# Two-layer cross-attention on one core: a logarithm in the softmax shift, and layer 0 features that arrive transposed

## Chip, cores and metric

The kernel runs on one core of a Trainium2 chip. The metric is the device time of one execution in microseconds (us), the median of several runs. All data are fp32. Products that must keep fp32 accuracy are made from a high part (rounded to the fp32r format) and a low part (the rest), in three matmul passes: high x low, low x high, high x high.

## What is computed

Sixteen batches of 256 tokens with 512 features and 16 heads of 32 features. Layer 0 attends from `x` to the 512 rows of the context and `x` together, then runs an MLP over the result. Layer 1 attends from the output of layer 0 to the normalised context. The two attentions are, cut to what matters:

```python
h = jnp.concatenate([x, latents], axis=1)            # layer 0: 512 keys
q = (latents @ q_w + q_b); kv = (h @ kv_w + kv_b)
attn = jnp.where(full_mask, einsum('bkhd,bnhd->bhkn', q, k) / DH, -inf)
attn_out = softmax(attn) @ v;  attn_out = attn_out @ out_w + out_b + residual
out = rmsnorm(attn_out, postnorm_w)                   # then the MLP and the residual
...
a = _layer_norm(audio_kv, ln_gamma, ln_beta)          # layer 1: 256 keys
out = softmax(Q @ K^T * scale) @ V @ Wo.T;  return hidden + tanh(gate) * out
```

## The kernel before

Three blocks follow one another: layer 0's attention, the MLP over 8 chunks of 512 tokens, layer 1's attention. Both attentions are the one function `attention_layer`. Each engine runs its own program in its written order, and semaphores tie them together. One round of the loop works on two batches at once: the first half of attention of batch `a` and the projections of the next batch `p = a + 1`. The batch before `a` is `prev`.

A round, in TensorE's order, is a row of slots and then the second pass.

- The slots hold the value products of `a` (`v_item`, `v_share`), the items of `p` (`item`) and, spread between their passes, the scores of `a` (`scores`, 32 in layer 0, each 128 queries of one head against 512 keys). The items of layer 0 are four transposes of tokens (`("tokens", f)`, four 128x128 transposes each, L1324), four key products and two query products. An item lands in one of two PSUM banks (`item_ps`). ScalarE copies its high part (`high`) and VectorE subtracts for the low part (`low`). The first two value tiles use the same two banks and are copied out by VectorE (`copy_v`, L1170) as each is made.
- Each score tile goes through a ring of four banks: VectorE takes the negative row maximum (`step_max`, L1106), ScalarE exponentiates with the row sum (`step_sum`, L831), and the score four later may then be written. In layer 0 the round starts with four scores ahead.
- For each half of the heads VectorE makes a `shift` tile (`make_shift`) of the negative maxima and of the reciprocal row sums, both as high and low parts; TensorE transposes it (`turn_shift`, L1448), ScalarE copies it (`copy_shift`, L837), and SyncE's DMA (L603) puts the maxima into two more rows of the `stack` tile, which holds keys and queries. `spread_sums` (L1460) multiplies a 0/1 matrix by the copied tile, so that every output feature sees the reciprocal sum of its head, and ScalarE copies that out (`copy_inv`, L845).
- The second pass takes the scores again, transposed and already shifted (`shifted`, L1475, 16 steps in layer 0 and 8 in layer 1, two halves of a ring), ScalarE exponentiates (`exps`, L852, five buffers), TensorE weighs the values (`weigh`, L1491; `run(g)` is four of these). VectorE multiplies by the reciprocal sums (`normalise`, L1126), `o_high` (L861) and `o_low` (L1132) split the result, and `project` multiplies by the output weights. Two of layer 0's items and four scores of the next batch lie between these steps.
- VectorE adds the residual (`finish`, L1150). In the next round ScalarE squares the rows (L871), GpSimd makes the scale (L738 to L743) and multiplies (L750), and TensorE transposes the result (`turn_norm`, L1518), which VectorE copies (L1163) for the MLP.

SyncE's queue holds, in this order: tokens of the batch after next, the shift rows of half 0, residual rows, the normalised result, the shift rows of half 1, and then 17 moves for each half of the next batch's `stack` (L557, L536); the moves of half 0 wait for the eighth `shifted` step. The features of the batch that is being worked on lie in one pair of tiles, `hT = feats`, so the features `f` of `p` can be written only when the value products of `a` have read features `f` (`v_shared`, and `v_done` for the last). The last round of layer 0 (`p` is None) also begins the MLP: GpSimd makes high parts (`ahead.highs`, L113 and L118), VectorE the low parts (`first_lows`, L107 and L127).

## Time and profile before

| | us |
|---|---|
| median of 3 runs (2361.79 to 2361.86) | 2361.8 |
| profiled execution, its span | 2367.1 |
| layer 0's attention, 0 to about | 1030 |
| one round of layer 0 in the loop | 62.07 |
| MLP, about 1030 to about | 1756 |
| one round of layer 1 in the loop | 37.60 |

In the page's 40 slices PE is at 9 tenths or more in nearly all, in the MLP and in both attentions; ScalarE is at 6 to 8 tenths in the attentions, VectorE at 5 to 7, GpSimd at 0 to 2. The chain of work that ended last names TensorE for 53% of the span and every other engine for 1% or less. The profiled execution is 5.3 us longer than the median.

### The profile page before, as it was taken

How to read it: one execution, taken by the hardware profiler on the slowest of the kernel's cores; microseconds unless marked ns; L12 is line 12 of the kernel's file. 1: busy time of each engine (PE TensorE's matmuls, PEld its weight loads, DVE VectorE, ACT ScalarE, POOL GpSimd, SP SyncE). 2: the span in 40 equal slices, each digit the busy share in tenths (PEclk: the TensorE clock that was granted, in tenths of full speed). 3: DMA queues.
4: the chain of work that ended last, by engine and by line, in shares of the span. 5: the costliest groups of instructions: out<-in, count | busy, mean ns of one | idle time of the engine just before them, and what ended most of it. 6: DMA issues, size and time to landing. Idle time of an engine off the chain costs nothing.

```text
span 2367.1 us, 44011 instructions
## 1 busy us (share of the span) xinstructions
PE 2333.6 (99%) x14706; PEld 1903.5 (80%) x14706; DVE 1160.4 (49%) x2246; ACT 1480.3 (63%) x3458; POOL 299.2 (13%) x336
## 2 busy tenths in 40 slices
PE   8999999999999999999999999999999999999998
PEld 7877777777777777678888888888878888888886
DVE  7555555555666566633122122122156666666664
ACT  6777777778777777744222222222248778787876
POOL 1111110111111110410000000000131221212120
PEclk9999999999999999999999999999999999999999
DMA  7444444444444444622011011011144555545443
GB/s 211 96 112 116 116 116 107 105 106 108 107 105 107 107 115 99 173 104 76 18 53 37 16 53 40 14 53 43 46 147 128 148 134 146 137 140 146 138 127 90
DMA packets 148369, 239.11 MB, mean 101 GB/s; under 512 B 25648, under 2 KB 59856, under 8 KB 148320
## 3 DMA queue, kind: packets, MB, share of 16 engines
q1 hardware_dynamic: 146912, 238.05, 37.0%
q10 hardware_dynamic: 1408, 0.41, 0.1%
q8 instruction: 30, 0.49, 0.1%
q14 instruction: 19, 0.16, 0.0%
HBM read 86.28 MB, written 25.21 MB: 47 GB/s over the span
## 4 chain that ended last, share of the span: by engine, by line
PE 53%; SPq 1%; ACT 1%; DMA 1%; DVE 0%; issue 0%; DVEq 0%
PE item_ps L65 6%; PE item_ps L66 6%; PE item_ps L67 6%; PE score_ps L67 5%; PE score_ps L66 5%; PE score_ps L65 5%; PE o_ps L65 4%; PE o_ps L67 4%; PE o_ps L66 4%; PE score_ps L1475 3%; PE score_ps L1434 2%; PE o_ps L1491 2%; SPq L536 1%; PE item_ps L1324 1%; ACT score_ps L831 1%; DMA layer_result<-rows 0%
## 5 line engine op out<-in xcount | busy, mean ns | idle before, releaser
L831 ACT ACTIVATE score_ps<-score_ps,l_neg_max 128x512 f32<-128x512 f32 (+1 forms) x1024 | 568.6, 561 | 121.5 <-DVE l_neg_max L1106 119.5
L1106 DVE TENSOR_REDUCE l_neg_max<-score_ps 128x1 f32<-128x512 f32 (+1 forms) x768 | 495.9, 684 | 56.9 <-PE score_ps L1434 55.4
L1947 ACT ACTIVATE mlp_hidden<-score_ps,b_col 128x512 f32<-128x512 f32 x128 | 88.4, 691 | 503.4 <-PE score_ps L67 457.9
L1995 DVE TENSOR_TENSOR mlp_hidden_l<-mlp_hidden,mlp_hidden_h 128x512 fp32r<-128x512 f32 x128 | 92.0, 719 | 519.2 <-ACT mlp_hidden_h L1949 519.1
L65 PE MATMUL item_ps<-feats_h,weights_l 128*128 128x256 f32 (+1 forms) x1024 | 322.0, 314 | 1.7 <-PEq L1821 0.8
L852 ACT ACTIVATE l_probs<-score_ps 128x1024 f32<-128x1024 f32 x272 | 270.8, 1020 | 82.1 <-PE score_ps L1475 79.0
L66 PE MATMUL item_ps<-feats_l,weights_h 128*128 128x256 f32 (+1 forms) x1024 | 318.2, 311 | 0.0
L67 PE MATMUL item_ps<-feats_h,weights_h 128*128 128x256 f32 (+1 forms) x1024 | 317.9, 310 | 0.0
L1434 PE MATMUL score_ps<-l_stack 97*128 97x512 f32 (+1 forms) x1024 | 299.8, 360 | 13.0 <-ACT score_ps L831 7.1
L1475 PEld LDWEIGHTS score_ps<-l_stack 99*128 99x128 f32 x1536 | 214.1, 193 | 49.4 <-issue 17.2
L1475 PE MATMUL score_ps<-l_stack 99*128 99x256 f32 x1536 | 244.9, 292 | 4.0 <-ACT score_ps L831 2.4
L1434 PEld LDWEIGHTS score_ps<-l_stack 97*128 97x128 f32 x1024 | 174.0, 190 | 56.8 <-ACT score_ps L831 34.1
L831 ACT ACTIVATION_READ_ACCUMULATOR score_ps<-score_ps,l_neg_max 128x1 f32 x1024 | 218.0, 213 | 0.0
L67 PEld LDWEIGHTS item_ps<-feats_h,weights_h 128*128 128x128 f32 x1024 | 194.1, 190 | 11.4
L65 PEld LDWEIGHTS item_ps<-feats_h,weights_l 128*128 128x128 f32 x1024 | 194.7, 190 | 10.2 <-DVE feats_l L1081 1.9
L66 PEld LDWEIGHTS item_ps<-feats_l,weights_h 128*128 128x128 f32 x1024 | 194.8, 190 | 9.2
L67 PE MATMUL score_ps<-feats_h,weights_h 128*128 128x512 f32 x512 | 201.6, 394 | 0.0
L66 PE MATMUL score_ps<-feats_l,weights_h 128*128 128x512 f32 x512 | 201.1, 393 | 0.0
L65 PE MATMUL score_ps<-feats_h,weights_l 128*128 128x512 f32 x512 | 199.3, 389 | 0.3 <-PEq L293 0.3
L1491 PE MATMUL o_ps<-l_probs,l_v 128*32 128x256 f32 x2176 | 137.3, 390 | 0.0
L1126 DVE TENSOR_TENSOR l_o_norm<-o_ps,norm_room 128x256 f32<-128x256 f32 x124 | 52.3, 422 | 145.4 <-PE o_ps L1491 145.4
L1906 POOL TENSOR_TENSOR rows<-rows,b_row 128x512 f32<-128x512 f32 x32 | 40.8, 1307 | 585.6 <-DMA rows<-in_x 585.6
(176 smaller groups left out, 4191.6 us busy)
## 6 DMA issues: line engine op xcount, KB each, us to landing
l_stack<-room SPq DMA_DIRECT2D x254, 192.0 KB, 3.2
l_stack<-l_qk SPq DMA_DIRECT2D x254, 128.0 KB
l_stack<-room SPq DMA_DIRECT2D x130, 128.0 KB, 2.9
l_stack<-l_qk SPq DMA_DIRECT2D x254, 64.0 KB
l_stack<-room SPq DMA_DIRECT2D x130, 64.0 KB, 2.9
l_tokens<-in_x SPq DMA_DIRECT2D x16, 512.0 KB, 3.4
l_tokens<-in_ctx SPq DMA_DIRECT2D x16, 512.0 KB, 4.3
l_rows<-in_x SPq DMA_DIRECT2D x16, 512.0 KB, 4.0
```

The source lines that it names most:

```text
L65: pe.matmul(out, left_l, right_h, start=start, stop=False)
L66: pe.matmul(out, left_h, right_l, start=False, stop=False)
L67: return pe.matmul(out, left_h, right_h, start=False, stop=stop)
L831: m = act.activation(e, e, ACT.Exp, bias=neg_max[:, q, h:h + 1], accum_out=row_sum[:, q, h:h + 1])
L852: act.activation(probs[s % PROBS].rearrange("p (a b) -> p a b", a=2), score_ps[:, 2 * (s % 2):2 * (s % 2) + 2, :], ACT.Exp).then_inc(probs ...
L1106: dve.tensor_reduce(out, bank, AXIS_X, ALU.max, negate=True).then_inc(max_done, 1)
L1126: dve.tensor_tensor(o_norm[:, g % 2, :], o_ps[g % 2][:, 0:S], inv_of(a)[:, g, :], ALU.mult).then_inc(o_norm_done, 1)
L1434: m = pe.matmul(out, rows[:, P * q:P * (q + 1)], rows[:, K_COLS], start=True, stop=True)
L1475: n = pe.matmul(score_ps[:, 2 * (s % 2) + j // 2, S * (j % 2):S * (j % 2 + 1)], stack[h // HALF][0:ROWS_ALL, h % HALF, S + P * kb:S + P * ...
L1491: n = pe.matmul(o_ps[g % 2][to, 0:S], v[:, kb, DH * h:DH * (h + 1)], probs[s % PROBS][:, S * j:S * (j + 1)], start=(kb == 0), stop=(kb == ...
L1947: act.activation(hidden[:, m % HBUF, :], hidden_ps[:, m % 4, :], ACT.Gelu_apprx_tanh, bias=b1_col[:, m:m + 1])
L1995: dve.tensor_tensor(hidden_p[1][:, m % HBUF, :], hidden[:, m % HBUF, :], f32(hidden_p[0][:, m % HBUF, :]), ALU.subtract).then_inc(hidden_l ...
```

## The change

- **Shift.** After the last row sum of each half ScalarE takes its logarithm (`ACT.Ln`). The shift tile becomes negative maximum minus that logarithm, as high and low parts, 16 rows in place of 32. The exponentials of the second pass are thereby normalised. `spread_sums`, `copy_inv` and `normalise` are gone, in both layers, and `o_high` and `o_low` read the PSUM bank. ScalarE is told to load a table set that has both functions.
- **Features of layer 0.** The host lays `x` and the context out transposed, one 1 MB block a batch, and one DMA loads it (`load_features`). GpSimd makes high and low parts (`split_tokens`). The 16 transposes a batch, ScalarE's `high` and VectorE's `low` of the token items are gone.
- **Slots of layer 0.** Value products are no longer taken tile by tile: four slots `("values", f)` hold the passes of three tiles for one `f` each, and the fourth tile is made whole at the end of the round before (`v_ahead`). All four value tiles are copied out by VectorE in slot 4, the first item slot. Five of the six items have slots; the sixth lies at the start of the second pass. Scores are spread 3 to a slot (once 4). In the second pass a run, two `shifted`, a `project`, two `shifted` and the next run follow one another.
- GpSimd normalises the rows of `prev` between the second and the third split. In the last round all low parts of the MLP's second unit stand ahead of `o_low(a, 0)` on VectorE. In layer 1 `turn_shift(a, 1)` stands one quarter of an item later.

```diff
-    NT, NK, NQ = FB, FB, (FB // 2 if first else 0)
+    NT, NK, NQ = (0 if first else FB), FB, (FB // 2 if first else 0)
...
-    INV_ROW = 2 * HALF
-    INV_LOW_ROW = INV_ROW + HALF
-    SHIFT_ROWS = INV_LOW_ROW + HALF
+    SHIFT_ROWS = 2 * HALF
...
-    MIXED = NT + NK - 1
-    SLOT = [("share", 0)] + [("v", t) for t in range(PLAIN_V)] + [("item", k) for k in range(MIXED)]
+    MIXED = 5 if first else NT + NK - 1
+    SLOT = ([("values", f) for f in range(FB)] if first else [("share", 0)]) + [("item", k) for k in range(MIXED)]
...
-    STEPS_AT_FIRST = [2, 4, 4, 2, 2, 2, 2, 3, 3, 2] if first else [2, 2, 2, 2, 2, 2, 2, 2]
-    STEPS_IN_SLOT = [3, 5, 5, 1, 1, 1, 1, 4, 4, 3] if first else [1, 1, 1, 1, 0, 3, 3, 2]
+    STEPS_AT_FIRST = [3, 3, 3, 3, 3, 3, 3, 3, 2] if first else [2, 2, 2, 2, 2, 2, 2, 2]
+    STEPS_IN_SLOT = [3, 3, 3, 3, 3, 4, 3, 3, 3] if first else [1, 1, 1, 1, 0, 3, 3, 2]
...
-    V_AHEAD = 1 if first else 2
-    TURN_SLOT = AFTER_T
-    NORM_SLOT = AFTER_T
-    VALUE_SLOT = AFTER_T - 2 if first else AFTER_T
-    V_OF_ACT = [PLAIN_V] if first else list(range(KB))
-    V_OF_DVE = KB - len(V_OF_ACT)
-    SHARE_BEHIND = {0: 2, 1: 3} if first else {1: 2, 2: 3}
...
+    V_AHEAD = FB if first else 2
+    V_ORDER = [PLAIN_V, PLAIN_V + 1, 0, 1] if first else [0, 1]
+    TURN_SLOT = AFTER_T + 1 if first else AFTER_T
+    NORM_SLOT = AFTER_T + 1
+    VALUE_SLOT = AFTER_T
+    SHARE_BEHIND = {} if first else {1: 2, 2: 3}
...
+        def load_features(sp, b):
+
+            at_least(sp, split_low_done, FB * b)
+            sp.dma_start(tokens, query_src[b]).then_inc(block_loaded, 16)
...
+                if first and a is not None and p is not None and not (isinstance(p, int) and p == B - 1):
+                    load_features(sp, p + 1)
...
+            def split_tokens(b, f):
+
+                pool.wait_ge(block_loaded, 16 * b + 16)
+                if not isinstance(b, int) or b > 0:
+                    if f < FB - 1:
+                        pool.wait_ge(v_shared, (FB - 1) * (b - 1) + f + 1)
+                    else:
+                        pool.wait_ge(v_done, KB * b)
+                pool.tensor_tensor(stat[:, :, 5], stat[:, :, 5], eps[:, :], ALU.mult)
+                pool.tensor_copy(hT[0][:, f, :], tokens[:, f, :]).then_inc(split_high_done, 1)
+                pool.wait_ge(split_high_done, FB * b + f + 1)
+                pool.tensor_tensor(hT[1][:, f, :], tokens[:, f, :], f32(hT[0][:, f, :]), ALU.subtract
+                                   ).then_inc(split_low_done, 1)
...
+            def normalise_rows(b):
+
+                pool.wait_ge(rstd_done, b + 1)
+                pool.tensor_tensor(stat[:, :, 4], stat[:, :, 2], eps[:, :], ALU.add)
+                for t in range(QT):
+                    n = pool.tensor_scalar(rows[:, t, :], rows[:, t, :], stat[:, t, 2:3], None, ALU.mult)
+                n.then_inc(norm_done, 1)
+
+            def iteration(p, a, prev):
                 if first and p is None:
+                    row_scale(prev)
+                    normalise_rows(prev)
                     ahead.highs(pool, v_done)
+                elif first and a is not None:
+                    split_tokens(p, 0)
+                    split_tokens(p, 1)
+                    if prev is not None:
+                        row_scale(prev)
+                        normalise_rows(prev)
+                    split_tokens(p, 2)
+                    split_tokens(p, 3)
...
+                if k % (STEPS // HALVES) == STEPS // HALVES - 1:
+                    half = k // (STEPS // HALVES)
+                    act.wait_ge(sum_done, STEPS * a + k + 1)
+                    act.activation(log_sum[:, half, :, :], row_sum[:, :, HALF * half:HALF * (half + 1)], ACT.Ln
+                                   ).then_inc(log_done, 1)
...
-            def copy_inv(a, half):
-                act.wait_ge(spread_done, HALVES * a + half + 1)
-                at_least(act, o_norm_done, FB * a)
-                if first and half == 0 and not last_of_first(a):
-                    at_least(act, stored, 16 * a)
-                act.activation(inv_of(a)[:, GROUPS * half:GROUPS * (half + 1), :].rearrange("p g s -> p (g s)"),
-                               o_ps[half][:, :], ACT.Copy).then_inc(inv_copied, 1)
...
             def o_high(a, g):
-                act.wait_ge(o_norm_done, FB * a + g + 1)
+                act.wait_ge(pv_done, PSTEPS * a + KB * (g + 1))
...
             def second_pass_of_two_keys(p, a):
                 exps(a, 0)
+                exps(a, 1)
                 copy_shift(a, 1)
-                exps(a, 1)
-                copy_inv(a, 0)
                 exps(a, 2)
-                copy_inv(a, 1)
                 exps(a, 3)
...
+            def second_pass_of_four_keys(p, a):
                 exps(a, 0)
                 exps(a, 1)
-                copy_inv(a, 0)
+                exps(a, 2)
                 copy_shift(a, 1)
-                exps(a, 2)
+                if p is not None:
+                    high(p, MIXED)
                 exps(a, 3)
-                copy_inv(a, 1)
-                for s in range(4, PSTEPS):
-                    exps(a, s)
-                    if s % KB == 2:
-                        o_high(a, s // KB - 1)
+                for g in range(FB - 1):
+                    o_high(a, g)
+                    for s in range(KB * (g + 1), KB * (g + 2)):
+                        exps(a, s)
                 o_high(a, FB - 1)
...
+                dve.wait_ge(log_done, HALVES * a + half + 1)
+                heads, log = slice(HALF * half, HALF * (half + 1)), log_sum[:, half, :, :]
+                high = shift[:, half, :, 0:HALF]
+                dve.tensor_tensor(log, neg_max[:, :, heads], log, ALU.subtract).then_inc(shift_step, 1)
+                dve.wait_ge(shift_step, 2 * (HALVES * a + half) + 1)
+                dve.tensor_copy(high.bitcast(F32R), log).then_inc(shift_step, 1)
+                dve.wait_ge(shift_step, 2 * (HALVES * a + half) + 2)
+                dve.tensor_tensor(shift[:, half, :, HALF:2 * HALF].bitcast(F32R), log, high, ALU.subtract
+                                  ).then_inc(shift_made, 1)
...
-            def normalise(a, g):
-
-                dve.wait_ge(pv_done, PSTEPS * a + KB * (g + 1))
-                dve.tensor_tensor(o_norm[:, g % 2, :], o_ps[g % 2][:, 0:S], inv_of(a)[:, g, :], ALU.mult
-                                  ).then_inc(o_norm_done, 1)
...
+                    if first and a is not None and slot == VALUE_SLOT:
+                        for t in range(KB):
+                            copy_v(a, t)
...
                         ahead.first_lows(dve)
-                    normalise(a, 0)
+                        for part in range(FB):
+                            ahead.parts.w1_low(dve, 1, part)
...
+            def tokens_split(b, f):
+
+                if first:
+                    pe.wait_ge(split_low_done, FB * b + f + 1)
+                else:
+                    pe.wait_ge(low_done, ITEMS * b + f + 1)
...
+            def values(b, f, step):
+
+                for t in V_ORDER[1:]:
+                    if f == 0 and t > PLAIN_V:
+                        at_least(pe, o_low_done, FB * b)
+                    elif f == 0:
+                        at_least(pe, rows_done, QT * (b - 1) + t + 1)
+                        pe.wait_ge(low_done, ITEMS * (b + 1) - PLAIN_V + 1 + t)
                     step()
                     n = v_passes(b, t, f)
-                n.then_inc(v_done, 1)
+                    if f == FB - 1:
+                        n.then_inc(v_done, 1)
+                if f < FB - 1:
+                    n.then_inc(v_shared, 1)
 
             def v_ahead(b):
 
                 pe.wait_ge(low_done, ITEMS * (b + 1))
-                pe.wait_ge(o_norm_done, FB * b - 1)
+                at_least(pe, o_low_done, FB * b - 1)
                 for f in range(V_AHEAD):
-                    v_passes(b, PLAIN_V, f)
+                    n = v_passes(b, PLAIN_V, f)
+                if V_AHEAD == FB:
+                    n.then_inc(v_done, 1)
 
             def v_share(b, f):
...
-            def spread_sums(a, half):
-
-                pe.wait_ge(shift_copied, HALVES * a + half + 1)
-                if last_of_first(a) and half == 0:
-                    values_copied(a + 1)
-                elif first and half == 0:
-                    at_least(pe, nT_done, a)
-                for g in range(GROUPS):
-                    n = pe.matmul(o_ps[half][:, S * g:S * (g + 1)], spread[:, g, :], shiftT[:, half, :],
-                                  start=True, stop=True)
-                n.then_inc(spread_done, 1)
...
+            def groups_of_four_keys(p, a, run, shifted):
+                run(0)
+                for g in range(1, FB):
+                    shifted(a, KB * g)
+                    shifted(a, KB * g + 1)
+                    if g == 1:
+                        items_free(p)
+                    project(a, g - 1)
+                    shifted(a, KB * g + 2)
+                    shifted(a, KB * g + 3)
+                    run(g)
...
-                    if q == 2:
+                    if q == 3 and not first:
                         turn_shift(a, 1)
-                        spread_sums(a, 0)
-                    if q == 3:
-                        spread_sums(a, 1)
...
+    turned = np.stack([inputs["x"], inputs["ctx_2048"]], axis=1).reshape(B, 2 * S, FB, P).transpose(0, 3, 2, 1)
+    arrays["in_features"] = np.ascontiguousarray(turned)
+    tensors["features"] = nc.dram_tensor("in_features", turned.shape, F32, kind="ExternalInput").ap()
```

## Rows read from the trace of the kernel before

**Rows 1.** The page, first part: busy time of TensorE (matmuls) over the span.

```profile
PE 2333.6 (99%) x14706; PEld 1903.5 (80%) x14706; DVE 1160.4 (49%) x2246; ACT 1480.3 (63%) x3458; POOL 299.2 (13%) x336
```

**Rows 2.** Windows: length; busy us PE, PEld, DVE, ACT, POOL; clock; DMA share; GB/s.

```profile
488.58:550.65 62.07, 61.73 (x426) 48.92 (x425) 36.42 (x70) 48.72 (x106) 7.31 (x9) 1.00 0.44 111
968.50:1024.96 56.46, 50.49 (x307) 34.18 (x307) 36.27 (x65) 40.95 (x89) 23.21 (x21) 0.88 0.43 127
1977.90:2015.50 37.60, 37.60 (x298) 32.59 (x296) 24.68 (x55) 30.46 (x91) 6.81 (x8) 1.00 0.52 141
```

**Rows 3.** Timeline of TensorE, layer 0 slots: start, us, line, out<-in, count.

```profile
483.12 0.60 PE L1324 MATMUL item_ps<-ident,l_tokens 128*128 128x128 f32 x4
...
483.79 0.39 PE L65 MATMUL o_ps<-weights_h,feats_l 128*128 128x512 f32 x1
484.02 0.40 PE L66 MATMUL o_ps<-weights_l,feats_h 128*128 128x512 f32 x1
...
504.34 0.48 PE L1460 MATMUL o_ps<-l_shiftT,l_spread 128*128 128x256 f32 x2
504.66 0.40 PE L65 MATMUL item_ps<-feats_h,weights_l 128*128 128x512 f32 x1
```

**Rows 4.** Timeline of TensorE, second pass of layer 0.

```profile
517.44 1.93 PE L1491 MATMUL o_ps<-l_probs,l_v 128*32 128x256 f32 x32
519.30 1.22 PE L1475 MATMUL score_ps<-l_stack 99*128 99x256 f32 x8
```

**Rows 5.** Timeline of GpSimd: row scale, row product, cast, tensor-tensor.

```profile
537.06 0.19 POOL L738 TENSOR_TENSOR l_stat<-l_stat,l_per_row 128x2 f32<-128x2 f32 x1 [21.86 <-ACT norm_room L871]
...
538.94 3.12 POOL L750 TENSOR_SCALAR l_rows<-l_rows,l_stat 128x512 f32<-128x512 f32 x2
...
991.24 2.29 POOL L118 CAST feats_h<-room 128x512 fp32r<-128x512 f32 x4 [3.61 <-PE o_ps L67]
...
1910.26 2.53 POOL L719 TENSOR_TENSOR room<-room,ln_gamma 128x512 f32<-128x512 f32 x2 [1.12 <-DVE room L1072]
```

**Rows 6.** Timeline of VectorE: maxima, residual add, value copy.

```profile
531.46 2.48 DVE L1106 TENSOR_REDUCE l_neg_max<-score_ps 128x1 f32<-128x512 f32 x4 [0.30 <-PE score_ps L1434]
534.24 1.29 DVE L1150 TENSOR_TENSOR l_rows<-item_ps,l_rows 128x512 f32<-128x512 f32 x2 [0.30 <-PE item_ps L67]
...
542.05 0.68 DVE L1170 COPY l_v<-item_ps 128x512 f32<-128x512 f32 x1
```

**Rows 7.** Timeline of ScalarE, second pass of layer 0.

```profile
513.24 1.94 ACT L852 ACTIVATE l_probs<-score_ps 128x1024 f32<-128x1024 f32 x2 [1.85 <-PE score_ps L1475]
515.07 0.51 ACT L861 ACTIVATE l_oT_h<-l_o_norm,l_bv 128x256 fp32r<-128x256 f32 x1
```

**Rows 8.** The page, sixth part: DMA issues, last number us to landing.

```profile
l_stack<-room SPq DMA_DIRECT2D x254, 192.0 KB, 3.2
```

**Rows 9.** Timeline of SyncE's queue: stack moves of half 0, shift rows of layer 1.

```profile
516.58 10.68 SPq L536 DMA_DIRECT2D l_stack<-room  x16
...
2050.82 1.43 SPq L603 DMA_DIRECT2D l_stack<-l_shiftT  x2
```

**Rows 10.** Timeline of TensorE in that round of layer 1.

```profile
2055.10 1.10 PE L1475 MATMUL score_ps<-l_stack 99*128 99x256 f32 x7
```

**Rows 11.** Timeline of the last round of layer 0: VectorE and GpSimd for the MLP.

```profile
995.94 3.08 DVE L107 SCALAR_TENSOR_TENSOR weights_l<-room,norm_w,weights_h 128x512 fp32r<-128x512 f32 x4
...
993.51 7.47 POOL L113 TENSOR_SCALAR weights_h<-room,norm_w 128x512 fp32r<-128x512 f32 x4
```

**Rows 12.** Windows at a pause of TensorE in the first round of layer 0.

```profile
35.27:38.68 3.41, 1.78 (x8) 1.18 (x7) 3.27 (x5) 1.66 (x6) 0.00 (x0) 1.00 0.86 190
38.68:42.09 3.41, 3.41 (x10) 2.62 (x9) 1.64 (x3) 2.72 (x8) 0.00 (x0) 0.50 0.96 205
```

**Rows 13.** Timeline: the first key pass, and ScalarE's table load.

```profile
13.00 0.50 PE L65 MATMUL item_ps<-feats_h,weights_l 128*128 128x512 f32 x1
...
2.36 1.28 ACT L808 ACT_TABLE_LOAD   x1 [2.36 <-issue]
```

411 lines of the change are left out of this document (143 added, 268 removed).

## The prediction

> **What bounds the kernel now.** I read the page first: TensorE's matmuls are busy for 99% of the span [rows 1]. That alone proves little, since a matmul's recorded duration overlaps the next one, so I turned to the timeline. There a pass of 512 columns starts 0.23 us after the one before it although its record lasts 0.39 [rows 3], a pass of 256 columns half of that later, and this pace holds through slots, second pass and MLP. The windows give a layer 0 round 62.07 us and a layer 1 round 37.60 us, both full [rows 2]. Counted at that pace, a layer 0 round is: 120 passes of 512 for items, values and projections and 32 scores, 35.1; 48 passes of 256 for queries, 5.8; 64 `shifted` matmuls, 7.5; four runs at 1.86 [rows 4], 7.4; transposes of norm and shift, 1.1; about 1.1 of switching between kinds; token transposes and `spread_sums`, 2.3. That is 60.3, so 1.8 us of a round are real gaps. In such a kernel removed TensorE work comes off the end at full price, unless the order of the other engines opens new gaps. ScalarE (48.7 of 62) and VectorE (36.4) have room on average; GpSimd with 7.3 us looks free [rows 2]. An average over a round says nothing on the few microseconds in which one of them has to deliver, and that is where this change has to be read.
>
> **What is removed.** Four token transposes and a score take 0.67 us from start to the next pass [rows 3]; without the score's 0.23, 0.44 a group, four groups, 1.78 a round of layer 0. Two spread matmuls cost 0.32 and the other pair 0.24: 0.56 a round, both layers. ScalarE loses seven copies and VectorE four multiplies and four subtractions in layer 0; both lay beside TensorE's work, worth nothing directly.
>
> **New gap 1, slot 4.** Time 0 is the start of a layer 0 round. A `values` slot is 9 passes and 3 scores, 12 x 0.23 = 2.77 us, so slots 0 to 3 end at 11.1. Item 0 of `p` follows and needs all four features split.
>
> GpSimd's split of one `f` can begin when the slot of that `f` has ended. It is a small operation 0.17, a cast at 2.29 / 4 = 0.57 plus a semaphore 0.1, and a subtraction of two SBUF tiles, for which the nearest row is the 1.26 of a tensor-tensor (2.53 / 2): 2.2 us in all [rows 5]. Between splits 1 and 2 stands the row scale, 538.94 - 537.06 = 1.9, and the row product, 3.1: 5.0 us [rows 5]. Split 0: 2.9 to 5.1. Split 1 waits for slot 1: 5.7 to 7.9. Norm: to 12.9. Split 2: to 15.1. Split 3: to 17.2. The squares that the norm waits for are done near 3, so they are not late. Queued behind on GpSimd is only the residual bias, which nobody needs before the end of the round.
>
> Item 0's bank also holds value tile 0, which VectorE now copies only in slot 4, behind that slot's first maximum: score ready 11.5, maximum 0.61, copy 0.68 [rows 6], so the first pass starts at 12.8 rather than 11.3. Features 0 and 1 then run to 14.7, feature 2 waits until 15.1, feature 3 until 17.2. The slot ends at 17.9 instead of 14.6: **3.4 us**. If the subtraction were no dearer than the cast it would be about 1.6, which is the bank's wait alone; with every GpSimd step a tenth slower, 4.7. I take 3.4, since three of four GpSimd prices are rows of the same shape.
>
> **New gap 2, second pass.** Items used to lie between `shifted` steps and runs; now one does. ScalarE's exponentials come at 0.95 (1.94 for two) and an `o_high` at 0.46 to 0.51 [rows 7]. At `run(0)` ScalarE still has the shift copy and the two query copies (each like an `o_high`) ahead of `exps(3)`, which ends about 2.4 us after `shifted(3)`, while three quarters of a run take 1.4: 0.9. In each of the three groups after it, counted from the end of the last run: `o_high` to 0.7, two exponentials to 2.6, but `project` can start only at 1.2 (after `o_low`) and pushes `shifted` step 3 to 2.6; its exponentials end at 3.3 + 1.9 = 5.2, the last quarter of the run at 5.7. TensorE's own work is four `shifted` 1.9, a project 1.4, a run 1.9 and the switches, 5.3. So 0.4 each, 1.2 for three. I leave out the bounds below zero: fewer items cannot make this stretch faster than its own work.
>
> **New gap 3, the stack.** The moves of half 0 wait for `shifted(7)`: it ends at 44.9 by the times above. From there the 17 moves take 0.8 + 10.7 [rows 9], and the last lands 3.2 after issue at most [rows 8], at 58.9 to 59.1. The next scores want it at 58.5: 0.4 (0 to 1).
>
> Other waits move with no cost: the feature DMA waits for split 3 and stands ahead of the shift rows, which come later (23); rows and norm have their old place.
>
> **Sum of a layer 0 round.** -1.8 - 0.6 - 1.8 (old gaps, which a row of items behind a pause hides) + 3.4 + 0.9 + 1.2 + 0.4 = +1.7; walking through the slots one by one gives 64.1 against 62.07, +2.0. I take +1.9, 14 rounds: **+26.6**. The first round has no norm on GpSimd, so only the bank's wait: 0. The start: ScalarE's weight splits no longer stand behind token copies, and the first key pass at 13.00 [rows 13] comes about 1 us sooner, of which the load of weights leaves 0.8: **-0.8**. The last round (56.46 [rows 2]): its first pass ends 1.3 sooner, the second pass is three groups of 5.7, but `o_low(0)` now stands behind 12 low parts (4 x 0.77 [rows 11] and so on), the last four of which wait for GpSimd's 7.5 us [rows 11]; I get 52.5: **-4**.
>
> **Layer 1.** -0.56 a round. Against it, `turn_shift(1)` comes a quarter later, after `shifted(2)`: copy done at 2051.9 in the times of the profiled round, two issues of 0.7 [rows 9], landing 2.3 to 2.9 after the second starts, 2054.9 to 2055.5, while `shifted(4)`, at 2055.10 before [rows 10], would want to start at 2054.6: 0.3 to 0.9. `v_ahead` now waits for `o_low(2)` rather than `normalise(2)`: 0.2. Net 0.1 a round, 15 rounds, and the tail loses 1: **+1**, between -8 and +10.
>
> **Time.** -0.8 + 26.6 - 4 + 1 = +22.8 on the profiled span of 2367.1; the median lies 5.3 below its span, and I put the same difference on it: 2361.8 + 22.8 = **2385**.
>
> **Rivals.** (1) *Only the bank's wait decides.* GpSimd delivers in time; slot 4 costs 1.6 and a round +0.1: -0.8 + 1.4 - 4 + 1, 2359. For it: GpSimd's average load. Against: the serial 13.7 us that must fit between 2.9 and 14. (2) *TensorE's work decides*, the other side: neither GpSimd's splits nor the second pass is late. It decides as soon as features are ready by 14 and value copies by 11.3; then only part of the old gaps stays, a round is about 60.6, -1.5: 2361.8 - 0.8 - 21 - 4 - 1 = 2335, and 2316 if layer 1 gains its whole 0.56 and all gaps of layer 0 close too. (3) *The clock.* After a stretch in which TensorE was busy 1.78 of 3.41 us, the granted clock was 0.50 for the next 3.41 us, that is 1.2 in place of 2.4 GHz, and a pass took twice as long [rows 12]. The pauses of slot 4 are alike. If every round fell to the low clock once, that is 1.7 us x 14: 2408. Against: such a stretch must fall just so, and the rounds drift. (4) *It doesn't do what it says*: the logarithm is not in the loaded table set, and each `Ln` swaps tables twice, 1.28 us each [rows 13], 64 times: about 2385 + 64 x 1.5 = 2480. The Trainium skill speaks against this one: "ScalarE: Activation LUTs", section "Table sets: the hidden batching unit", says one set holds both exponential and logarithm, so one load serves; no row of before shows a logarithm, so this stays open until the profile. The same skill has a rule against the change: "GPSIMD Engine Reference", key points, puts VectorE at about twice GpSimd's speed for elementwise work; the trace agrees, 1.26 us against 0.61 to 0.69 for 128x512, and it is what makes gap 1.
>
> **How the numbers follow.** Forecast 0.56; clock 0.08; tables 0.02; rival 1 0.12; rival 2 0.22. Slower by over 0.2% (above 2366.5; about what a measurement of this kernel tells from no change) is the first three, 0.66; within 0.2% 0.12; faster 0.22. The likeliest case alone reaches from 2370 (gap 1 at 2.6, layer 1 at -8) to 2402. The range takes in rival 1, most of rival 2 and the clock: 2335 to 2408.
>
> **What would show it.** Right: TensorE idle before an L65 pass of the first key item, released by GpSimd's subtraction, and a round near 64; one pause of about 1.5 before it, released by VectorE's value copy; pauses in the second pass released by L852. In layer 1, `shifted(4)` waiting for the DMA of the shift rows. One table load per block. Wrong: a round under 62, GpSimd's last split done before TensorE asks, or half-clock windows in every round.

## The result, and the profile after

The changed kernel takes 2434.3 us against 2361.8 us of the kernel before: ratio 1.0307, 95% interval 1.0292 to 1.0321. Forecast were 2385 us and a range up to 2408. The sign was right, the size was not: 72.5 us lost where I had 23. The profiled execution has a span of 2438.1 us, 71.0 more than that of before; its four executions took 2431.5 to 2439.9 us, and the profiled one is the longest.

Where the 71 us lie is read from the windows. I cut both spans at the same four places: the first transposes of the norm, the fourteenth, the last, and layer 1's first product. First the kernel before, then the changed one (length; busy us of TensorE's matmuls, its loads, VectorE, ScalarE, GpSimd; granted clock; DMA share; GB/s).

```profile
0.00:115.87 115.87, 108.37 (x650) 88.44 (x650) 73.71 (x116) 80.81 (x167) 14.99 (x23) 0.96 0.58 154
115.87:923.05 807.18, 802.56 (x5514) 635.66 (x5513) 473.32 (x898) 633.30 (x1366) 94.98 (x117) 1.00 0.44 111
923.05:1030.49 107.44, 101.34 (x676) 74.03 (x674) 60.41 (x116) 78.23 (x160) 27.23 (x27) 0.94 0.39 107
1030.49:1742.13 711.64, 710.37 (x3119) 579.37 (x3119) 155.14 (x235) 197.94 (x323) 48.16 (x43) 1.00 0.14 49
1742.13:2367.10 624.97, 610.94 (x4752) 526.03 (x4752) 397.86 (x884) 490.04 (x1444) 113.83 (x127) 0.99 0.50 137
```

```profile
0.00:126.82 126.82, 107.95 (x607) 83.66 (x608) 68.29 (x99) 75.05 (x156) 39.70 (x56) 0.96 0.53 141
126.82:985.48 858.66, 801.00 (x5253) 604.77 (x5252) 424.18 (x754) 601.93 (x1300) 199.07 (x273) 1.00 0.42 104
985.48:1095.24 109.76, 101.21 (x659) 72.47 (x657) 55.19 (x99) 76.49 (x155) 25.81 (x27) 0.91 0.39 104
1095.24:1801.89 706.65, 705.30 (x3119) 579.49 (x3119) 154.66 (x235) 197.62 (x323) 48.59 (x43) 1.00 0.14 49
1801.89:2438.10 636.21, 611.17 (x4688) 523.39 (x4688) 356.99 (x756) 483.00 (x1445) 106.96 (x123) 0.98 0.54 135
```

The transposes of the norm stand 1.5 us later within a round than before (18.38 us behind the start of the last projection's last pass, against 16.84), so the first and third rows are not whole rounds. Cut at that pass instead, which starts at 99.03, 968.26 and 1024.73 us before and at 108.45, 1032.74 and 1089.46 us in the changed kernel, the stages fit the terms of the forecast:

| stage | forecast | measured |
|---|---|---|
| start and first round | -0.8 | +9.4 |
| 14 rounds of layer 0 (62.09 to 66.02 us each) | +26.6 | +55.1 |
| last round of layer 0 (56.46 to 56.72 us) | -4 | +0.3 |
| feed-forward stage | 0 | -5.0 |
| layer 1 | +1 | +11.2 |

So 48 us were missed: 28.5 in the rounds of layer 0, 10 at the start, 10 in layer 1 and 4 in the last round, less 5 that nothing in the forecast gave.

ScalarE and VectorE have less to do than before in the second window row, as the change promises; TensorE idles. In [rows 2] a round was 61.73 of 62.07 busy; now it is 61.56 of 66.00:

```profile
589.75:655.75 66.00, 61.56 (x405) 46.50 (x404) 32.65 (x58) 46.30 (x100) 15.32 (x21) 1.00 0.43 104
```

What TensorE waits for (total, times, longest), the first lines of the waits of the changed kernel:

```profile
PE item_ps L66 <- POOL feats_l L699: 21.9, 17, 5.1
PE item_ps L66 <- DVE l_v L1142: 20.4, 14, 1.5
PE o_ps L1449 <- ACT l_probs L865: 9.7, 15, 0.6
PE score_ps L1407 <- DMA l_stack<-l_qk: 9.4, 10, 3.4
PE score_ps L1407 <- DMA l_stack<-room: 7.1, 14, 1.3
```

Slot 4 of one round, TensorE, then GpSimd and VectorE in the same microseconds; the bracket is the idle time before and what ended it:

```profile
582.99 0.39 PE L1407 MATMUL score_ps<-l_stack 97*128 97x512 f32 x1
584.84 0.49 PE L66 MATMUL item_ps<-feats_h,weights_l 128*128 128x512 f32 x1 [1.46 <-DVE l_v L1142]
...
588.94 0.51 PE L66 MATMUL item_ps<-feats_h,weights_l 128*128 128x512 f32 x1 [1.06 <-POOL feats_l L699]
```

```profile
578.50 1.30 POOL L699 TENSOR_TENSOR feats_l<-l_tokens,feats_h 128x512 fp32r<-128x512 f32 x1
579.76 0.19 POOL L726 TENSOR_TENSOR l_stat<-l_stat,l_per_row 128x2 f32<-128x2 f32 x1
...
581.63 3.11 POOL L739 TENSOR_SCALAR l_rows<-l_rows,l_stat 128x512 f32<-128x512 f32 x2
...
587.62 1.26 POOL L699 TENSOR_TENSOR feats_l<-l_tokens,feats_h 128x512 fp32r<-128x512 f32 x1
```

```profile
583.42 0.69 DVE L1087 TENSOR_REDUCE l_neg_max<-score_ps 128x1 f32<-128x512 f32 x1 [0.23 <-PE score_ps L1407]
584.03 1.28 DVE L1142 COPY l_v<-item_ps 128x512 f32<-128x512 f32 x2
```

Both pauses of slot 4 are there and in the order that was forecast. With time 0 at 571.6, as there, the last split ends at 17.3 (17.2 was forecast), the slot ends at 18.15 (17.9), and the copy's pause ends at 13.2 (12.8). The subtraction of two SBUF tiles takes 1.26 to 1.30, as the tensor-tensor of [rows 5].

The second pass, ScalarE and then TensorE:

```profile
608.24 2.87 ACT L865 ACTIVATE l_probs<-score_ps 128x1024 f32<-128x1024 f32 x3
611.49 0.37 ACT L856 ACTIVATE l_shiftT<-o_ps 16x256 fp32r<-16x256 f32 x1 [0.38 <-PE o_ps L1418]
611.77 0.80 ACT L836 ACTIVATE room<-item_ps,l_bq 128x256 fp32r<-128x256 f32 x2
612.48 1.00 ACT L865 ACTIVATE l_probs<-score_ps 128x1024 f32<-128x1024 f32 x1
```

```profile
613.53 0.64 PE L1449 MATMUL o_ps<-l_probs,l_v 128*32 128x256 f32 x8 [0.65 <-ACT l_probs L865]
```

The fourth exponential stands behind shift copy and query copies; TensorE waits 0.65 us within its first run.

### The profile page after: what moved, and what is told of

It reads as the page before. It is cut to its first block, busy times and chain, and to the rows that moved or that the text cites. A ratio compares the mean times of both kernels' runs of the same rounds, so it can differ in the third digit from the quotient of the medians.

```text
span 2438.1 us, 42636 instructions
## 1 busy us (share of the span) xinstructions
PE 2326.6 (95%) x14322; PEld 1863.8 (76%) x14322; DVE 1059.3 (43%) x1942; ACT 1434.1 (59%) x3378; POOL 420.1 (17%) x521
## 4 chain that ended last, share of the span: by engine, by line
PE 40%; SPq 10%; DMA 2%; issue 1%; ACT 1%; DVE 0%; DVEq 0%
SPq L531 9%; PE item_ps L66 5%; PE item_ps L68 5%; PE item_ps L67 5%; PE score_ps L67 5%; PE score_ps L66 5%; PE score_ps L68 5%; PE o_ps L66 3%; PE o_ps L68 3%; PE o_ps L67 3%; PE score_ps L1407 2%; DMA l_stack<-l_qk 1%; PE score_ps L1433 1%; SPq L599 1%; SPq L552 0%
## 5 line engine op out<-in xcount | busy, mean ns | idle before, releaser
L66 PE MATMUL item_ps<-feats_h,weights_l 128*128 128x256 f32 (+1 forms) x1024 | 329.6, 322 | 47.4 <-POOL feats_l L699 21.9
L1407 PE MATMUL score_ps<-l_stack 97*128 97x512 f32 (+1 forms) x1024 | 308.7, 360 | 23.4 <-DMA l_stack<-l_qk 9.4
L865 ACT ACTIVATE l_probs<-score_ps 128x1024 f32<-128x1024 f32 x272 | 264.9, 1021 | 59.8 <-PE score_ps L1433 59.5
L1433 PEld LDWEIGHTS score_ps<-l_stack 99*128 99x128 f32 x1536 | 208.8, 192 | 54.1 <-issue 23.3
L845 ACT ACTIVATION_READ_ACCUMULATOR score_ps<-score_ps,l_neg_max 128x1 f32 x1024 | 212.4, 207 | 0.0
L67 PEld LDWEIGHTS item_ps<-feats_l,weights_h 128*128 128x128 f32 x1024 | 195.7, 191 | 10.4
L1449 PE MATMUL o_ps<-l_probs,l_v 128*32 128x256 f32 x2176 | 148.6, 389 | 15.5 <-ACT l_probs L865 9.7
L1104 DVE SCALAR_TENSOR_TENSOR l_oT_l<-o_ps,l_bv,l_oT_h 128x256 fp32r<-128x256 f32 x64 | 30.9, 483 | 280.9 <-ACT l_oT_h L874 280.9
```

The lines of the kernel that those rows point to most:

```text
L66: pe.matmul(out, left_l, right_h, start=start, stop=False)
L67: pe.matmul(out, left_h, right_l, start=False, stop=False)
L845: m = act.activation(e, e, ACT.Exp, bias=neg_max[:, q, h:h + 1], accum_out=row_sum[:, q, h:h + 1])
L865: act.activation(probs[s % PROBS].rearrange("p (a b) -> p a b", a=2), score_ps[:, 2 * (s % 2):2 * (s % 2) + 2, :], ACT.Exp).then_inc(probs ...
L1407: m = pe.matmul(out, rows[:, P * q:P * (q + 1)], rows[:, K_COLS], start=True, stop=True)
L1433: n = pe.matmul(score_ps[:, 2 * (s % 2) + j // 2, S * (j % 2):S * (j % 2 + 1)], stack[h // HALF][0:ROWS_ALL, h % HALF, S + P * kb:S + P * ...
```

## The experiments

Each kernel was timed in turns with the kernel before on one chip; times in the text are its ratio times 2361.8 us, since the median of before was 2363 to 2365 us there. The changed kernel stands at 1.0307. The rows below are edits to the changed kernel, but for the two with the logarithm alone, which are edits to the kernel before. For a round of layer 0 I give the mean distance of the norm's first transposes over 13 rounds, for one of layer 1 the mean over the rounds in its middle. The start, and both ends of layer 1, differ by 2 or 3 us between the profiles of kernels that are alike there, so a stage of one profile says less than the ratio.

| kernel | ratio (95%) | round, layer 0 | round, layer 1 |
|---|---|---|---|
| before | 1 | 62.09 | 37.60 |
| changed | 1.0307 (1.0292 to 1.0321) | 66.05 | 37.70 |
| logarithm alone | 0.9953 (0.9937 to 0.9970) | 61.73 | 37.29 |
| the same with a pad | 0.9970 (0.9958 to 0.9982) | 61.71 | 37.25 |
| late-vector wait moved | 1.0279 (1.0261 to 1.0296) | 66.12 | 37.73 |
| copies first | 1.0339 (1.0322 to 1.0356) | 66.88 | 37.79 |
| row product behind the splits | 1.0185 (1.0168 to 1.0202) | 64.07 | 37.71 |
| both of these | 1.0115 (1.0099 to 1.0130) | 63.14 | 37.76 |
| layer 1's shift early | 1.0266 (1.0245 to 1.0287) | 66.11 | 37.31 |
| second pass reordered | 1.0258 (1.0239 to 1.0278) | 65.15 | 37.76 |
| all, product between the casts | 1.0371 (1.0351 to 1.0392) | 68.28 | 37.29 |
| the same and second pass | 1.0267 (1.0242 to 1.0292) | 66.88 | 37.28 |
| all mended, VectorE subtracts | 0.9923 (0.9909 to 0.9936) | 61.16 | 37.30 |
| all mended, GpSimd splits | 0.9936 (0.9922 to 0.9949) | 61.15 | 37.27 |
| and projection, tile 0 | 1.0055 (1.0041 to 1.0069) | 63.19 | 37.32 |
| and tile 0 alone | 0.9897 (0.9882 to 0.9913) | 60.69 | 37.32 |
| and rows sooner | 0.9946 (0.9933 to 0.9960) | 61.40 | 37.33 |

**One part alone.** The kernel before with the logarithm only: line L831 gets the new step, `spread_sums`, `copy_inv` and `normalise` go, features and slots stay.

```diff
+                if k % (STEPS // HALVES) == STEPS // HALVES - 1:
+                    half = k // (STEPS // HALVES)
+                    act.wait_ge(sum_done, STEPS * a + k + 1)
+                    act.activation(log_sum[:, half, :, :], row_sum[:, :, HALF * half:HALF * (half + 1)], ACT.Ln
+                                   ).then_inc(log_done, 1)
...
-            def spread_sums(a, half):
...
-            def normalise(a, g):
```

> The kernel before with the logarithm part alone, in both layers: no spreading of the inverse sums, no scaling of the outputs; features, slots and the orders of the second pass stay as before. My theory, taken from the prediction: this part is 0.56 us of TensorE work less in every one of 31 rounds, so about 17 us faster, 2345; if the 5 us that the feed-forward stage lost in the changed kernel come from the same memory layout, 2340. Rival: the freed time is eaten by waits of the second pass, within 3 us of 2362. A third reading: the logarithm is what made layer 1's ends slower, then layer 1 grows by 5 or more.

0.9953: 11 us faster, between theory and rival. A round gains 0.36 in layer 0 and 0.31 in layer 1 and not 0.56. The spread matmuls and the switches behind them did take 0.56, but other steps grew once they were gone. The step in front of the second shift's transposes went from 0.33 to 0.42 us in layer 0 and from 0.12 to 0.16 in layer 1; the rest lies in several steps of 0.1 us or less, and why they grow, no run shows. So one half of the change is a gain in this order, and what is lost comes with the other half, features and order, and with the place of layer 1's second shift.

The feed-forward stage took 706.6 us here too, as in the changed kernel. Its own work is the same in all three. What differs is a 4-byte tile: one that held the output of an activation was allocated ahead of the stage's tiles and is gone, and the activation that wrote it became a table load. The pad puts back the tile alone.

```diff
-            ("stat", [P, QT, 8]), ("gate", [P, 1]), ("tanh_gate", [P, 1]))}
+            ("stat", [P, QT, 8]), ("gate", [P, 1]), ("tanh_gate", [P, 1]), ("pad", [P, 1]))}
```

> The logarithm part alone, with one unused 4-byte-a-partition tile put back where the kernel before keeps its table output, so that the tiles of the feed-forward stage stand at the addresses of before. Theory: the 5.1 us that this stage lost (pitch of a 512-column pass 0.2303 to 0.2287 us) hang on the layout: the stage takes 711.6 again. Rival: the layout has nothing to do with it, the stage takes 706.6.

The stage takes 711.66 us again. Windows of 700 us inside it, before, logarithm alone, with the pad; TensorE is busy throughout, and what differs is how many matmuls (x) start in the same time:

```profile
1040.00:1740.00 700.00, 699.90 (x3066) 570.83 (x3065) 149.00 (x226) 192.64 (x314) 47.74 (x40) 1.00 0.13 46
```

```profile
1027.00:1727.00 700.00, 699.06 (x3090) 574.55 (x3088) 154.39 (x232) 195.35 (x320) 48.03 (x41) 1.00 0.14 49
```

```profile
1032.00:1732.00 700.00, 699.50 (x3069) 570.66 (x3067) 149.11 (x226) 191.79 (x312) 46.28 (x39) 1.00 0.13 46
```

**The start.** GpSimd has a wait for the late vectors ahead of its loop. Before, only the residual bias stood behind it; now the second batch's splits do.

```diff
             else:
-                pool.wait_ge(late_vec_loaded, 16 * (VECTORS - VECTORS_EARLY))
...
+                    if isinstance(a, int) and a == 0:
+                        pool.wait_ge(late_vec_loaded, 16 * (VECTORS - VECTORS_EARLY))
                     pool.wait_ge(rows_loaded, 16 * (a + 1))
```

(In the file the removed line is the last of the branch for layer 0.) The changed kernel's timelines of GpSimd and TensorE, of SyncE, and the window behind the pause:

```profile
52.25 0.19 POOL L696 TENSOR_TENSOR l_stat<-l_stat,l_eps 128x2 f32<-128x2 f32 x1 [30.33 <-DMA l_bo<-in_L_xattn_out_b]
...
54.47 0.77 PE L66 MATMUL item_ps<-feats_h,weights_l 128*128 128x512 f32 x1 [5.12 <-POOL feats_l L699]
```

```profile
35.38 10.79 SPq L531 DMA_DIRECT2D l_stack<-room  x16
...
47.92 0.56 SPq L654 DMA_DIRECT2D l_bo<-in_L_xattn_out_b  x1
```

```profile
54.08:64.32 10.24, 9.43 (x20) 6.11 (x21) 2.93 (x7) 3.02 (x7) 6.22 (x10) 0.50 0.25 89
```

> The changed kernel with one wait moved: GpSimd waits for the late vectors only ahead of the residual bias of the first batch, no longer ahead of the splits of the second batch's features. Theory: TensorE's 5.12 us pause at 49.4 and the 10.24 us at half clock behind it (5.1 more) both go: about 10 us less, 2424. Rival: another wait of the first round takes their place (the value copy of 1.5 us and the clock dip stay): 2430 to 2433.

The first norm transposes come at 117.69 in place of 126.82, 9.1 us sooner; the ratio gives 7 us where 10 were expected. The pause is the theory's. The half clock behind it (granted clock 0.50, 1.2 GHz) varies: it was 10.24 us long here and in one more profile with the wait in its old place, and 3.41 in four others, so the longest execution was profiled with a dear one.

**Slot 4.** Two edits, alone and together.

```diff
+                    if first and a is not None and slot == VALUE_SLOT:
+                        for t in range(2):
+                            copy_v(a, t)
                     for k in steps[:1]:
                         step_max(a, k)
```

> The changed kernel with VectorE copying value tiles 0 and 1 ahead of the first maximum of slot 4, so that the bank of the first key item comes free 1.4 us sooner. Theory: the last split of GpSimd decides when slot 4 ends, the 1.46 us pause for the copy lies inside that wait, so TensorE only waits longer at the later features: within 4 us of 2434, and the pause at GpSimd's subtraction grows from 1.1 to about 2.5 us. Rival: the pauses are independent and add up: 14 x 1.4 = 20 us less, 2414.

```diff
+                    split_tokens(p, 2)
+                    split_tokens(p, 3)
                     if prev is not None:
                         row_scale(prev)
                         normalise_rows(prev)
-                    split_tokens(p, 2)
-                    split_tokens(p, 3)
...
-    NORM_SLOT = AFTER_T + 1
+    NORM_SLOT = AFTER_T + 2
```

(`TURN_SLOT` of layer 0 moves by one slot too.)

> The changed kernel with GpSimd's row scale and row product (5.0 us) behind all four splits in place of between the second and third, and the transposes of norm and shift one slot later. Theory: the last split is then ready before TensorE asks, the 1.1 us pause and its switch of 0.2 to 0.3 go in 14 rounds, the copy's pause stays: 18 us less, 2416. Rival: the later norm and shift rows make a new wait (norm transposes or the shift rows' DMA), and nothing is gained.

> The changed kernel with both: tiles 0 and 1 copied first, and GpSimd's row product behind the splits. Alone the first made it 8 us slower and the second 28 us faster. Theory: the copy's 1.46 us counts in full only when no split is late behind it, so together they bring 28 and another 13 x 0.9 = 12 (0.5 of the pause is left, as in the mended kernels): 2396, a round of 63.1, and no half-clock windows in the loop. Rival: freeing the bank early pushes TensorE against the last split again, the round stays at 64.0 or dips: 2408 or more.

Copies first alone: 8 us slower. The one round without half clock takes 65.97, as the theory says, but eight stretches of 3.41 us in the loop ran at half clock, and a round that holds most of one takes 1.0 to 1.3 us more. TensorE in a disturbed round, and the windows around it:

```profile
586.23 0.49 PE L66 MATMUL item_ps<-feats_h,weights_l 128*128 128x512 f32 x1 [0.53 <-DVE l_v L1142]
...
589.19 0.50 PE L66 MATMUL item_ps<-feats_h,weights_l 128*128 128x512 f32 x1 [0.85 <-POOL feats_l L699]
...
591.23 0.50 PE L66 MATMUL item_ps<-feats_h,weights_l 128*128 128x512 f32 x1 [1.08 <-POOL feats_l L699]
```

```profile
588.41:591.82 3.41, 1.55 (x6) 0.99 (x7) 1.28 (x3) 1.45 (x4) 2.69 (x4) 1.00 0.00 0
591.82:595.23 3.41, 3.41 (x14) 2.92 (x13) 0.66 (x2) 0.69 (x1) 0.00 (x0) 0.50 0.84 274
```

The pauses for splits have moved together, TensorE is busy 1.55 of 3.41 us, and then runs at half clock. Neither of my two readings had that. The row product behind the splits brings 28.8 us by the ratios; I expected 18. Both together bring 45 (40 expected): the copies first cost 8 us alone and give 17 here, so the copy's pause counts only when no split is late behind it. The round of 63.14 was expected at 63.1, and no loop round of this kernel ran at half clock.

**Layer 1's second shift, turned where it was before.**

```diff
-                    if q == 3 and not first:
+                    if q == 2 and not first:
                         turn_shift(a, 1)
```

ScalarE's copy moves with it. SyncE's queue in the last full batch, the changed kernel and then the kernel before:

```profile
2382.61 1.41 SPq L599 DMA_DIRECT2D l_stack<-l_shiftT  x2
2384.07 7.74 SPq L531 DMA_DIRECT2D l_stack<-l_qk  x12
```

```profile
2314.03 1.42 SPq L603 DMA_DIRECT2D l_stack<-l_shiftT  x2
2315.49 7.73 SPq L536 DMA_DIRECT2D l_stack<-l_qk  x12
```

> The changed kernel with layer 1's second shift turned and copied where the kernel before has it, after the second shifted step. Theory: the later turn holds up the queue of SyncE, whose 28 stack moves behind the shift rows come 2 us later; only the first and the last batch of layer 1 show it (pauses of 1.7 and 3.4 us and half clock behind them): 4 to 6 us less, the steady layer 1 round stays within 0.1 of 37.70. Rival: the steady round gains 0.3 or more, 10 us less. Second rival: layer 1's ends are slower for another reason and nothing changes.

9.7 us faster, the first rival: the steady round falls to 37.31, as with the logarithm alone. In the changed kernel the shift rows go out 11.9 us after the round's first shift transposes (2370.71), in the kernel before 10.4 us after (2303.66). The twelve stack moves stand behind them in the queue, and the waits for `l_stack<-l_qk` fall from 10 with 9.4 us to:

```profile
PE score_ps L1407 <- DMA l_stack<-l_qk: 6.5, 4, 3.4
```

**The second pass.** ScalarE makes the fourth exponential ahead of the item's copies, and a projection is cut in two.

```diff
                 exps(a, 2)
-                copy_shift(a, 1)
+                exps(a, 3)
                 if p is not None:
                     high(p, MIXED)
-                exps(a, 3)
+                copy_shift(a, 1)
...
-                    project(a, g - 1)
+                    project(a, g - 1, (0,))
                     shifted(a, KB * g + 2)
+                    project(a, g - 1, (1,))
                     shifted(a, KB * g + 3)
```

> The changed kernel with only layer 0's second pass reordered: ScalarE makes the fourth exponential before the last item's copies, and a projection's two halves stand on both sides of a shifted step. Theory: ScalarE's order costs 0.5 + 0.8 before and in the first run and 0.55 in each later group; up to the last shifted step of half 0 1.9 us go, and the stack moves start so much sooner; the 1.1 us of the last two groups are swallowed by the wait for the stack: 1.9 x 14 = 27 us less, 2409, and the wait for the stack's DMA grows from 0.5 to 1.6. Rival: the whole 3.0 go, 42 us less. Second rival: no gain, the splits of SyncE's queue or slot 4 take it up.

The round falls by 0.9, 12 us where 27 were expected. The wait for the stack grew from 0.48 to 1.42 us a round, near the theory's 1.6; of the 1.9 us that the theory gains before half 0's last shifted step only half survives that wait.

```profile
PE score_ps L1407 <- DMA l_stack<-room: 21.4, 15, 1.8
```

**All together, the row product still between the casts.** Here VectorE makes the subtraction of each split, the values of the next batch stand ahead of its scores, and the edits above are in: late vectors, copies first, layer 1's shift. The second kernel has the second pass reordered too. Neither moves the row product.

```diff
+                    if first and a is not None and p is not None and 1 <= slot <= FB:
+                        subtract_split(p, slot - 1)
```

> The changed kernel with every pause of slot 4 taken away together: late-vector wait moved, value tiles 0 and 1 copied first, VectorE subtracts the features' low parts so that GpSimd only casts, layer 1's shift turned early, values ahead of the next scores. Theory: in a layer 0 round the pauses of 1.6 and 1.2 us in slot 4 and the 0.9 us before the next scores go, with no half-clock windows: 3.7 x 14 = 52, and 7 for the late vectors, 5 for layer 1: about 64 us less than the changed kernel, 2372. Rival: VectorE, now with four more subtractions of 0.6 us in slots 1 to 4, delivers maxima late and TensorE waits for score banks: round above 64, 2400 or more.

> Everything of the last two together. Theory: a layer 0 round is TensorE's own 57.3 us and 1 to 2 us of switches and small waits, 59.0: 66.05 - 59.0 = 7 x 14 = 98 us less in layer 0, 12 elsewhere: about 2328 to 2335, faster than the kernel before. Rival: stack moves (17 x 0.67 us a half from the last shifted step of the half on) set the round: no shorter than 61, 2360.

Both are far from what was expected: 1.0371 and 1.0267 are 2449 and 2425 us, against 2372 and 2328 to 2335. VectorE in slots 3 and 4 of the first:

```profile
655.95 0.69 DVE L1097 TENSOR_REDUCE l_neg_max<-score_ps 128x1 f32<-128x512 f32 x1 [0.22 <-PE score_ps L1422]
659.86 0.69 DVE L1085 TENSOR_TENSOR feats_l<-l_tokens,feats_h 128x512 fp32r<-128x512 f32 x1 [3.21 <-POOL feats_h L699]
...
661.66 1.28 DVE L1152 COPY l_v<-item_ps 128x512 f32<-128x512 f32 x2
```

GpSimd's row product had stayed between its casts, and what had been GpSimd's lateness now held VectorE's queue: maxima and value copies stood behind the subtraction, and with them ScalarE's exponentials. TensorE paused 3.8 us in every round and ran at half clock behind it.

**All mended.** With the row product behind the casts, or GpSimd's whole splits:

> The last kernel with GpSimd's row scale and product moved behind its four casts (and the transposes of norm and shift a slot later). Its trace showed why it was slow: VectorE's third subtraction waited 3.2 us for a cast that stood behind the row product, and the copies that free the first item's bank stood behind the subtraction. Theory: with the casts first nothing in slot 4 waits, no half-clock windows, a layer 0 round of 57.3 us of work and 1.5 to 2.2 us of switches, 58.8 to 59.5: about 7 x 13 = 91 us less than the changed kernel in the loop and 20 elsewhere, 2320 to 2330, faster than the kernel before. Rival: VectorE's four extra subtractions make maxima late, 61 a round, 2350.

> The same, but with GpSimd making the whole splits as in the changed kernel. Theory: without the row product between them GpSimd ends the last split 2.2 to 2.8 us after slot 3, at 13.9, when TensorE asks at 14.1, so this is as fast as the kernel with the subtractions on VectorE, within 5 us; the norm is then ready at 18.9, up to 0.4 us late for its transposes. Rival: TensorE waits for the last split again (0.5 or more a round, 8 us) and GpSimd is the engine that sets slot 4 in any order.

0.9923 and 0.9936, that is 2344 and 2347 us, faster than the kernel before and some 3.7% below the changed one, but not the 2320 to 2330 that I expected. These kernels also hold an edit that has no run of its own, the next batch's values ahead of its scores. Who subtracts makes no difference that the intervals tell: the subtraction takes 0.69 us on VectorE and 1.30 on GpSimd, and in both orders it is ready in time. The round is 61.15 and not 59: 0.7 us are left in front of the first item (0.54 for the copy) and 0.5 in front of the second value tile (0.33 for the row sums).

> The kernel with all orders mended and GpSimd's whole splits, and two orders more: value tile 0 copied ahead of the last maximum of slot 3 (it takes away the 0.54 us pause before the first item), and the last projection with the row sums ahead of the next scores (it takes away the 0.33 us pause before the second value tile). Theory: each pause goes with its switch, 0.6 and 0.4 us, a layer 0 round of 60.1 to 60.2: 14 us less than 2349, 2335. Rival: the scores now come 1.4 us later, ScalarE's sums of slot 0 are late and score banks with them: the round stays at 61.1.

> The mended kernel with GpSimd's splits, plus only the copy of value tile 0 ahead of slot 3's last maximum; the last projection stays behind the next scores. Theory: of the run before, the copy took the 0.70 us pause away and the moved projection alone made the wait for ScalarE's sums of 1.9 us; so a round of 60.4 to 60.5, no half-clock windows in the loop, 9 us less than the mended kernel: 2340. Rival: the delayed maximum makes a wait for a score bank and the round stays at 61.1.

> The same with VectorE adding the residual rows ahead of the fourth maximum of the next batch in place of behind it. Theory: the 0.33 us pause before the second value tile and its switch go, 0.45 x 14 = 6 us less: 2334; the delayed fourth maximum costs up to 0.2 us at slot 1. Rival: that wait is larger than what is gained, as with the projection, 2340 or more.

```diff
                     for k in steps[1:]:
+                        if first and slot == VALUE_SLOT - 1 and k == steps[-1]:
+                            copy_v(a, 0)
                         step_max(a, k)
```

```diff
                 v_ahead(p)
+                project(a, FB - 1)
                 for k in range(AHEAD):
                     next_scores(p, k)
```

```diff
                     for k in range(AHEAD):
+                        if first and k == AHEAD - 1:
+                            finish(a)
                         step_max(p, k)
```

(Tile 0's copy, in all three kernels; the projection, in the first, where the row sums also stand ahead of all four maxima; the row sums ahead of the fourth alone, in the third.)

The copy of tile 0 ahead of one maximum gives the fastest kernel, 0.9897: 2337.5 us, 24 us below before and 97 below the changed kernel, also faster than the logarithm alone. Its round and its waits:

```profile
541.24:601.92 60.68, 59.83 (x404) 46.99 (x405) 33.85 (x59) 46.40 (x101) 15.41 (x21) 1.00 0.45 113
```

```profile
PE score_ps L1412 <- DVE l_rows L1123: 4.7, 14, 0.3
PE score_ps L1438 <- ACT l_probs L866: 4.5, 14, 0.3
```

Some 5 of the 24 us are the feed-forward stage's and come with the missing tile, not with the order. The last 0.33 us resists: with the projection ahead of the scores (2375 us, 2335 expected), or the row sums ahead of the fourth maximum (2349, 2334 expected), TensorE waits for ScalarE's sums instead, as I read it because that batch's exponentials start later. With the projection a round takes 62.45, or 63.8 where it holds a stretch at half clock, which is every second one.

```profile
PE score_ps L1415 <- ACT score_ps L846: 31.7, 22, 2.2
```

```profile
PE score_ps L1415 <- ACT score_ps L846: 13.8, 22, 2.2
```

(Projection ahead, then row sums ahead; in the fastest kernel it is 4.7 us.)

## Why the prediction was right in its mechanisms and wrong in its sum

**A round of layer 0: 1.9 forecast, 4.0 measured.** I laid the pitches of the prediction, the times from the start of one matmul to the start of the next, over both rounds: 0.231 us for 512 columns, 0.12 for 256, 1.86 for a run, and summed what is over. Before: work 59.3, over 2.7, of which 0.85 in single places of more than 0.12 us, the rest spread thin. Changed: work 57.3, over 8.8, of which 6.4 in single places. Term by term (the forecast's terms add to 1.8 here and to 1.7 as it rounded them; it took 1.9, toward the 2.0 of its slot-by-slot count):

| term | forecast | measured |
|---|---|---|
| removed TensorE work | -2.3 | -2.1 |
| old gaps that vanish | -1.8 | -0.85 |
| slot 4 | +3.4 | +2.85 |
| first run and around | +0.9 | +1.4 |
| three groups behind it | +1.2 | +1.1 |
| wait for the stack | +0.4 | +0.9 |
| others (0.19 in slot 0, thin rest) | 0 | +0.7 |

The new gaps sum to 6.4 with the 0.19 of slot 0, against 5.9. What failed is the step "1.8 us of a round are real gaps", which a row of items behind a pause hides. It came from a difference of two large sums, 62.07 less 60.3, and no row showed such gaps. In the trace of before, single places make up 0.85 of it. The rest is in steps too short to be a wait for another engine. The 136 undisturbed passes of 512 columns a round follow at 0.2319 us, which is 0.1 us a round over the pitch that I used. But 21 passes of 512 or 256 columns a round are followed 0.03 to 0.12 us late, most where one kind of matmul gives way to another or just behind such a place; together 2.0 us, where the prediction counted 1.1 for switching. The changed kernel pays these too: 25 places, 2.4 us. So 0.85 and not 1.8 went away, and the thin rest grew by 0.5: 1.4 of the 2.1 us missed in each round.

Slot 4 was sized well (its two pauses alone; the steps right behind them, some 0.1 us each, are in the thin rest), but as a cause it weighs more than its terms: the row product behind the splits gave back 2.0 us a round where the last split's pause is 1.25. By the two traces the rest is short steps again: 0.3 behind the first pass of three features, and 0.4 around the transposes of norm and shift.

**The start: -0.8 forecast.** The first key pass does come sooner, 11.38 against 13.00 [rows 13]. Missed is the wait for the late vectors. The prediction listed what is queued behind GpSimd's splits, not what stands in front of them in the first batch: 5.1 us, and half clock behind it. With the wait moved the first round ends at 99.26, 0.2 us behind that of before, so this one wait is nearly the whole 9.4.

**The last round of layer 0: -4 forecast, +0.3.** I had its work and not its pauses. TensorE waits 2.13 us for one of ScalarE's sums, which stands behind VectorE's four value copies:

```profile
1049.70 0.80 PE L1407 MATMUL score_ps<-l_stack 97*128 97x512 f32 x1 [2.13 <-ACT score_ps L845]
```

It also runs 20.48 us at half clock where before had 10.24 and 3.41, but that is not what decides: with only layer 1's shift moved it was 13.66 us, and the round still took 56.98. With the logarithm alone, in the old order, it takes 54.22, so the new order of this round costs about 2.5 us; no run takes that apart further.

**Layer 1: +1 forecast, +11.2.** The steady round was forecast at +0.1 and measured at +0.10, which is luck: the removal gives 0.3 and not 0.56, and the later shift costs 0.4. I had priced the shift by its own DMA, ahead of `shifted(4)` [rows 10]. TensorE waits for that DMA only three times, at the ends; in the steady rounds the turn acts through the stack moves queued behind it on SyncE, and the next batch's score waits for them. Over the whole of layer 1 the profiles of the six kernels with the later turn have 630 to 636 us and those of the ten with the early one 621 to 628, against 625.0 before. So the turn is worth some 9 of the 11 us. The last batch alone would mislead: it takes 37.73 in the changed kernel and 35.74 with the shift early, but 35.9 to 36.5 in the other five kernels with the later turn. The rest, 2 to 3 us either way between kernels that don't touch layer 1, goes along with half-clock stretches at both ends and stays open.

**The feed-forward stage: 0 forecast, -5.0.** Shown to come with the 4-byte tile: the pad brings all of it back.

**The rivals.** That only the bank's wait decides is out: GpSimd's chain had its pause in 14 rounds. That TensorE's work decides is out for this order; the mended kernels show where it becomes true, with features ready and values copied in time, and a round of 60.69 against the 60.6 that this rival gave. That closeness is partly luck: the rival reached 60.6 by gaps left from the old order, and what is left are the short steps and two waits of 0.33 and 0.32 us that it didn't name. The clock: in the changed kernel every loop round is at full clock; its 1.2 GHz stretches are at the start, in the last round of layer 0 and at both ends of layer 1. The rival came true in the experiments, where a pause grew or two moved together. Tables (the rival took 1.5 us for each logarithm where two loads of [rows 13] would be 2.6, and gave no row for it): the trace has four table loads in all, at 0.74, 1092.58, 1797.42 and 1801.60, against three before. By the Trainium skill, "ScalarE: Activation LUTs", section "Table sets: the hidden batching unit", logarithm and exponential share one set, and the trace agrees.

## What to carry to other kernels

Where a transfer of work to an idle engine is priced, list what stands ahead of it in that engine's queue in every batch, the first too, and let the part that others wait for go first; the order of two steps on GpSimd was worth 29 us here, and moving the dependent half to another engine only moved the wait to a worse queue. What a pause is worth depends on what is late behind it: the same copy moved forward cost 8 us alone and gave 17 once the splits were in time. Take pauses away in the order of the chain, and look at the granted clock whenever two come close. Call nothing a gap that no row shows: half of this difference of two large sums was short steps where one kind of matmul follows another, and they don't go away behind a pause.
